# A graph network's edge stage on one core: rings and loop body of eight groups instead of four, the loads of P divided differently over two queues

## The reference

```
ef  = silu(concat(h[row], h[col], edge_attr) @ edge_w1 + edge_b1)
ef  = silu(ef @ edge_w2 + edge_b2)
agg = segment_sum(ef * edge_mask, row)
h   = h + (silu(concat(h, agg) @ node_w1 + node_b1) @ node_w2 + node_b2)
```

## Time and profile before

| | |
|---|---|
| median of 3 runs | 8981.45 us (8978.94 to 8988.67) |
| the profiled execution | 9007.83 us, span 9006.1 us |
| TensorE (PE) busy | 6678.6 us, 74% of the span |
| GpSimd (POOL) busy | 5100.8 us, 57% |
| VectorE (DVE) busy | 5014.9 us, 56% |
| ScalarE (ACT) busy | 2799.6 us, 31% |
| first and last `first` of L1 (L1515) | start at 2367.5 and 6357.6 us |

### The profile page before, as it was taken

The page is one execution under the profiler, slowest core; times in us unless marked ns, Lnnn a source line. Parts: engine busy times, 40 slices in busy tenths (PEclk is TensorE's granted clock), DMA queues, the critical chain, the costliest instruction groups (busy, mean ns, idle before and its releaser), DMA issues. The chain is left out here.

```text
span 9006.1 us, 230609 instructions
## 1 busy us (share of the span) xinstructions
PE 6678.6 (74%) x51782; PEld 5543.5 (62%) x51783; DVE 5014.9 (56%) x13561; ACT 2799.6 (31%) x8299; POOL 5100.8 (57%) x7138
## 2 busy tenths in 40 slices
PE   1222226767799978999799988999766666888998
PEld 1111114555577757777577767878455555786998
DVE  6333346867355545555455545555322222998999
ACT  1222204544233323333233322333133333222554
POOL 3777736755366636666366645666167776221554
PEclk8555555555799989999899999999655555998999
DMA  2000004433366646666455555666311000332232
GB/s 63 3 3 3 3 29 138 119 100 110 110 166 165 164 112 165 165 166 164 107 164 164 164 121 159 169 166 167 90 31 7 7 7 6 78 82 57 73 72 60
DMA packets 1288626, 877.60 MB, mean 97 GB/s; under 512 B 448518, under 2 KB 1192859, under 8 KB 1287640
## 3 DMA queue, kind: packets, MB, share of 16 engines
q1 hardware_dynamic: 991510, 618.55, 25.3%
q0 software_dynamic: 134272, 178.98, 9.3%
q10 hardware_dynamic: 162752, 78.98, 3.1%
HBM read 832.60 MB, written 50.91 MB: 98 GB/s over the span
## 5 line engine op out<-in xcount | busy, mean ns | idle before, releaser
L1472 POOL DMA_INDIRECT qg<-q_tab,qidx x2520 | 2393.5, 950 | 1444.0 <-DVE qidx L1602 736.5
L1607 DVE COPY ps<-b 128x384 f32<-128x384 f32 x1120 | 628.2, 561 | 1640.7 <-ACT h L1581 1609.1
L1067 PE MATMUL ps<-rhs_i,ohi 128*128 128x128 f32 (+2 forms) x8640 | 1215.1, 266 | 209.8 <-issue 198.0
L1067 PEld LDWEIGHTS ps<-rhs_i,ohi 128*128 128x128 f32 (+1 forms) x8640 | 998.8, 162 | 340.3 <-issue 281.2
L1033 POOL COPY near<-x 128x48 bf16 x2160 | 675.7, 351 | 788.4 <-PE ps L1056 432.9
L1542 PE MATMUL ps<-ohm,h 128*128 128x128 f32 x6720 | 1001.1, 285 | 146.6 <-DVE ps L1607 136.6
L1195 POOL DMA_INDIRECT got_m<-y_tab,idx_m x832 | 815.5, 980 | 474.2 <-issue 251.7
L1517 PE MATMUL ps<-oht,pb 128*128 128x128 f32 x6720 | 1060.5, 295 | 0.0
L1574 ACT ACTIVATE h<-ps,b 128x384 f32<-128x384 f32 x1120 | 650.2, 581 | 1292.6 <-PE ps L1522 1245.2
L1542 PEld LDWEIGHTS ps<-ohm,h 128*128 128x128 f32 x6720 | 842.0, 192 | 281.5 <-issue 275.7
L1581 ACT ACTIVATE h<-ps 128x384 f32<-128x384 f32 x1120 | 549.1, 490 | 1432.5 <-PE ps L1531 1343.5
(11 more groups left out here) (438 smaller groups left out, 8629.8 us busy)
## 6 DMA issues: line engine op xcount, KB each, us to landing
pb<-p_tab SPq DMA_DIRECT2D x2240, 64.0 KB
places<-place_by_turn SPq DMA_DIRECT2D x560, 192.0 KB
places_i<-place_by_meeting SPq DMA_DIRECT2D x360, 256.0 KB, 3.4
places_i<-place_by_meeting SPq DMA_DIRECT2D x720, 128.0 KB, 3.1
pb<-p_tab ACTq DMA_DIRECT2D x1120, 64.0 KB
qb<-q_tab SPq DMA_DIRECT2D x840, 64.0 KB
qg<-q_tab,qidx POOLq DMA_INDIRECT x2520
eat<-rows_by_turn SPq DMA_DIRECT2D x560, 54.0 KB
```

The lines of the kernel that those rows point to most:

```text
L1067: m = pe.matmul(ps[:, bass.ds(to[j], width)], ohi[:, h, j, :], rhs[:, h, j, 0:width], start=False, stop=True, skip_group_check=True)
L1472: pool.indirect_dma_start(qg[:, h, j, :], None, q_tab, IndirectOffsetOnAxis(ap=qidx[:, h, j:j + 1], axis=0)).then_inc(m_got[h], 16)
```

## The change

The rings of `edge_mlp` and its loop body get eight slots (`U3` = 8, 35 rounds instead of 70); the other stages keep `U` = 4. The waits follow: a load may run up to eight groups ahead. SP loads all three blocks of P of the even group of a pair, ScalarE all three of the odd one (before: four on SP, two on ScalarE), and ScalarE's `fetch` runs six groups ahead instead of two, with three fetches ahead of its first step. The indices are copied five groups ahead instead of three. `nears` is loaded for both groups of a pair in one transfer, also for the group that doesn't use it. TensorE's address load for `sums` moves out of `sums` to the head of the even step, ahead of `first`. The sizes and counts are those of before.

```diff
+U3 = 8
-K3 = G3 // U
+K3 = G3 // U3
...
-                return 3 if h == NONE else 2
+                return 3 if h % 4 == 3 else 2
+            def blocks(q):
+                return 2 - q % 2
...
-                qg = sb(f"qg{layer}", [P, U, M3, HID], F32, st)
-                pb = sb(f"pb{layer}", [P, U, M3, HID], F32, st)
+                qg = sb(f"qg{layer}", [P, U3, M3, HID], F32, st)
+                pb = sb(f"pb{layer}", [P, U3, M3, HID], F32, st)
...
@@ gpsimd, gather
-                            if here(k, h, U):
-                                pool.wait_ge(m_z1, g0 + n - U + 1)
+                            if here(k, h, U3):
+                                pool.wait_ge(m_z1, g0 + n - U3 + 1)
...
@@ sync, fetch
-                                sp.wait_ge(m_z1, g0 + n - 2)
+                                sp.wait_ge(m_z1, g0 + n - U3 + 2)
...
-                            for i in range(2 - q):
-                                sp.dma_start(nears[:, h + i, :], near_p[bass.ds((n + i) * M3 + 2, 1), :].to_broadcast([P, P])).then_inc(m_pl[q], 16)
+                            sp.dma_start(nears[:, h:h + 2, :],
+                                         near_p[bass.ds(n * M3, 2 * M3), :].rearrange("(a g j) p -> a g j p", a=1, j=M3)[:, :, 2, :].to_broadcast([P, 2, P])).then_inc(m_pl[q], 16)
...
-                            sp.dma_start(pb[:, h + 1, 0, :], p_tab[bass.ds(at[4], P), :]).then_inc(m_sp[q], 16)
...
@@ tensor
-                            pe.wait_ge(m_sp[q], 16 * (7 - q) * (k0 + k + 1))
-                            pe.wait_ge(m_act[q], 32 * (k0 + k + 1))
+                            pe.wait_ge(m_sp[q], 16 * (4 + blocks(q)) * (k0 + k + 1))
+                            if h % 2:
+                                pe.wait_ge(m_act[q], 48 * (k0 + k + 1))
...
@@ tensor, sums
-                            if h % 2 == 0:
-                                to[:] = address(mybir.EngineType.PE, to_p[0:1, bass.ds(k * 2 + h // 2, 1), :].rearrange("a g j -> a (g j)"), (NB - 1) * P)
...
+                        def take(k, h):
+                            to[:] = address(mybir.EngineType.PE, to_p[0:1, bass.ds(k * (U3 // 2) + h // 2, 1), :].rearrange("a g j -> a (g j)"), (NB - 1) * P)
...
                         def step(k, h):
+                            if h % 2 == 0 and here(k, h, 2):
+                                take(*moved(k, h, -2))
                             first(k, h)
...
@@ scalar, fetch
-                                act.wait_ge(m_z1, g0 + n - 2)
-                            at = address(mybir.EngineType.Activation, at_p[0:1, bass.ds(n + 1, 1), 1:3].rearrange("a g j -> a (g j)"), (NB - 1) * P)
-                            for j in range(2):
-                                act.dma_start(pb[:, h + 1, 1 + j, :], p_tab[bass.ds(at[j], P), :]).then_inc(m_act[q], 16)
+                                act.wait_ge(m_z1, g0 + n - U3 + 2)
+                            at = address(mybir.EngineType.Activation, at_p[0:1, bass.ds(n + 1, 1), 0:4].rearrange("a g j -> a (g j)"), (NB - 1) * P)
+                            for j in range(M3):
+                                act.dma_start(pb[:, h + 1, j, :], p_tab[bass.ds(at[j], P), :]).then_inc(m_act[q], 16)
...
@@ scalar, step
-                                fetch(*moved(k, h, 2))
-                        fetch(0, 0)
+                                fetch(*moved(k, h, 6))
+                        for h in (0, 2, 4):
+                            fetch(0, h)
...
@@ vector, step
-                            indices(*moved(k, h, U - 1))
+                            indices(*moved(k, h, 5))
```

More of the change, by code:

```diff
@@ L26 @@
 M3 = 3
+U3 = 8
 G3 = NT // M3
-K3 = G3 // U
+K3 = G3 // U3
 GW = M3 * P
-NONE = U - 1
-NA = K3 * NONE
+NA = G3 // 4 * 3
 assert NA <= NT - NB * (NB - 1)
@@ L925, in _, with turns @@
                         dve.tensor_copy(to_p[0:1, hs, 0:6], banks[3][0:1, 0:HN].rearrange("a (g j) -> a g j", j=6)).then_inc(c_blk, 1)
-        def turns(eng, step, rounds=K):
+        def turns(eng, step, rounds=K, ring=U):
             for k in (0, 1):
-                for h in range(U):
+                for h in range(ring):
                     step(k, h)
             with eng.Fori(2, rounds - 1) as k:
-                for h in range(U):
+                for h in range(ring):
                     step(k, h)
-            for h in range(U):
+            for h in range(ring):
                 step(rounds - 1, h)
@@ L1430, in gnn_kernel @@
             sem("m_" + n) for n in ("idx", "oht", "ohm", "z1", "h1", "z2", "h2", "sum", "seed"))
-        m_got = [sem(f"m_got{h}") for h in range(U)]
-        m_pl, m_sp, m_act = ([sem(f"m_{n}{q}") for q in range(2)] for n in ("pl", "sp", "act"))
+        m_got = [sem(f"m_got{h}") for h in range(U3)]
+        m_pl, m_sp, m_act = ([sem(f"m_{n}{q}") for q in range(U3 // 2)] for n in ("pl", "sp", "act"))
         Z1, Z2 = 3584, NP
@@ L1440, in here, with moved @@
             def here(k, h, lag=0):
-                return there(k, h, lag, G3)
+                return not isinstance(k, int) or lag <= k * U3 + h < G3
             def gathered(h):
-                return 3 if h == NONE else 2
-            with ExitStack() as st:
-                qidx = sb(f"qidx{layer}", [P, U, M3], I32, st)
-                qg = sb(f"qg{layer}", [P, U, M3, HID], F32, st)
-                pb = sb(f"pb{layer}", [P, U, M3, HID], F32, st)
[L1450 to L1455, removed]
+                return 3 if h % 4 == 3 else 2
+            def blocks(q):
+                return 2 - q % 2
+            def moved(k, h, by):
+                d, slot = divmod(h + by, U3)
+                return (k + d if d else k), slot
+            with ExitStack() as st:
+                qidx = sb(f"qidx{layer}", [P, U3, M3], I32, st)
+                qg = sb(f"qg{layer}", [P, U3, M3, HID], F32, st)
+                pb = sb(f"pb{layer}", [P, U3, M3, HID], F32, st)
+                qb = sb(f"qb{layer}", [P, U3, HID], F32, st)
+                places = sb(f"places{layer}", [P, U3, GW], BF16, st)
+                nears = sb(f"nears{layer}", [P, U3, P], BF16, st)
+                eat = sb(f"eat{layer}", [36, U3, GW], BF16, st)
+                oht = sb(f"oht{layer}", [P, U3, GW], F32, st)
+                ohn = sb(f"ohn{layer}", [P, U3, P], F32, st)
                 ohm = sb(f"ohm{layer}", [P, 2, M3, P], F32, st)
@@ L1473, in gather @@
                                                         IndirectOffsetOnAxis(ap=qidx[:, h, j:j + 1], axis=0)).then_inc(m_got[h], 16)
-                        turns(pool, gather, K3)
+                        turns(pool, gather, K3, U3)
                     @block.sync
@@ L1491, in fetch @@
                             at = address(mybir.EngineType.SP, at_p[0:1, bass.ds(n, 2), :].rearrange("a g j -> a (g j)"), (NB - 1) * P)
-                            for i in range(2 - q):
+                            for i in range(blocks(q)):
                                 sp.dma_start(qb[:, h + i, :], q_tab[bass.ds(at[4 * i + 3], P), :]).then_inc(m_sp[q], 16)
@@ L1495, in fetch @@
                                 sp.dma_start(pb[:, h, j, :], p_tab[bass.ds(at[j], P), :]).then_inc(m_sp[q], 16)
-                            sp.dma_start(pb[:, h + 1, 0, :], p_tab[bass.ds(at[4], P), :]).then_inc(m_sp[q], 16)
                         sp.wait_ge(c_three, 48)
-                        turns(sp, fetch, K3)
+                        turns(sp, fetch, K3, U3)
                     @block.tensor
@@ L1551, in step @@
                                 second(*moved(k, h, -1))
[L1552 to L1555, removed]
+                        turns(pe, step, K3, U3)
+                        take(K3 - 1, U3 - 2)
+                        sums(K3 - 1, U3 - 2)
+                        second(K3 - 1, U3 - 1)
+                        sums(K3 - 1, U3 - 1)
                     @block.scalar
@@ L1576, in two @@
                         def two(k, h):
-                            n = k * U + h
+                            n = k * U3 + h
                             if here(k, h, 2):
@@ L1587, in step @@
                             if h % 2 == 0:
-                                fetch(*moved(k, h, 2))
-                        fetch(0, 0)
-                        turns(act, step, K3)
-                        two(K3 - 1, U - 2)
-                        two(K3 - 1, U - 1)
+                                fetch(*moved(k, h, 6))
+                        for h in (0, 2, 4):
+                            fetch(0, h)
+                        turns(act, step, K3, U3)
+                        two(K3 - 1, U3 - 2)
+                        two(K3 - 1, U3 - 1)
                     @block.vector
@@ L1633, in step @@
                             build(*moved(k, h, 1))
-                            indices(*moved(k, h, U - 1))
+                            indices(*moved(k, h, 5))
                             if here(k, h, 1):
                                 build_m(*moved(k, h, -1))
-                        for h in range(U - 1):
```

(5 more changed lines are left out.)

38 lines of the change are left out of this document (19 added, 19 removed).

## The result

The changed kernel takes 9034.11 us (median of 4 runs, 9029.61 to 9043.84), the kernel before 8983.93 us beside it (4 runs, 8978.94 to 8988.67). The ratio is 1.0057, 95% interval 1.004 to 1.0075: 50 us slower. The forecast was 8954, 80 us less than measured.

What follows compares the result with a forecast made beforehand. TensorE, and what makes it wait, was taken to set the time. Steady rounds +16, layer ends -6 and -4, last groups -34 gave -28 us against the profiled 9007.83, carried over to the runs' median as 8954 us; range 8890 to 9070.

Steps and rivals of the forecast that it cites:

- the load and some 0.1 us of register work fit in ... I take 0: TensorE's moved address load, 0.59 us, behind `second`: covered by 1.53 us of matmuls, so cost 0.
- The bound of the prediction, 317 us: TensorE's moved load if its cover were gone: at most 0.6 us twice a round, over 264 rounds.
- the gain of 34 us in the last groups: Layer ends: four more slots let TensorE run on during slow gathers, 8.5 us a layer gained, -34 us.
- Longer rings, the wait of 0.60 us a round goes.: Steady rounds, slot 0: with eight slots `first` no longer waits for rows of P, 0.60 us a round.
- ScalarE's third row, 0.33 us for each of two waits a round, 174 us.: ScalarE's fetch: third issue +0.51 us, shorter load -0.18, so two waits of 0.33 us more a round.
- Steady rounds, 13.20 us.: Rounds of four groups: 13.14 - 0.60 + 2 x 0.33 = 13.20 us, 0.06 slower, 264 times: +16 us.
- Ends of the layers.: Last six steps have no fetch, -6 us; at layer starts SP issues two transfers fewer first, -4 us.
- the first rival: ScalarE's fetch grows by more than 0.33 us: by 0.51 gives 9048 us, by 0.65 gives 9122, slower; chance 0.25.
- the third: Longer loop body's code fetched anew each turn: up to 290 us, with half of it 9100 us, slower; chance 0.06.
- The second: Slow gathers near layer ends are not helped, the crowd is there whatever the ring: 8988 us, same; chance 0.12.
- The fourth: Lateness taken up: ScalarE's third issue doesn't hold `two` back, round 12.54 us, 8779 us in all, much faster; chance 0.10.

## Why the prediction was wrong

The step that failed is "the load and some 0.1 us of register work fit in ... I take 0", on the address load of TensorE that was moved ahead of `first`. The cover, 1.53 us of matmuls, was counted from the start of `sums`, as if the sequencer came to the load at that time. It comes there, in program order, only after it has sent off `second`: 0.5 to 0.7 us after the start of `sums` in slots 2, 4 and 6, and 1.0 us after it where the loop has jumped back. `first` starts 0.9 to 1.0 us after the load at the earliest. In slots 2, 4 and 6 that just fits; at the head it doesn't. There the interval is 0.40 us longer than with the load back (4.11 against 3.71 us in the first layer, 4.0 against 3.6 in the others), at 128 heads some 51 us, and undoing it gave 68 us by the ratios and 54 by the traces. The bound of the prediction, 317 us, was for all even slots; one in four of them pays, and pays two thirds of 0.6 us. That the jump back is what brings the sequencer to the load half a microsecond later is shown, since slot 0 of the turn written straight out has no such delay. What in the jump takes that time stays open: the records have only an ALU operation of 0.036 us just ahead of the load. It is no fetching of code, since the queues that bring instructions moved nothing from 2450 to 3250 us of the changed kernel. And without a load behind it the jump costs nothing that TensorE's matmuls don't cover.

The second step that failed is the gain of 34 us in the last groups; it is the fifth point below.

The rest, in the prediction's order:

- *Longer rings, the wait of 0.60 us a round goes.* Right; no `first` waits for a transfer in steady rounds. With the other two parts undone this is worth 1.9% of the kernel before, 166 us by the medians; 264 x 0.60 is 158, and the steady rounds of the two traces differ by 0.59 us. The 0.60 came out of a division that was a little off: a round without waits was put at 11.53 us, and where nothing waits (ScalarE's rows between `two` and `one`) it takes 11.65, because slot 3 takes 2.91 us too in spite of its missing pass. So the waits in `sums` had 0.89 us of a round and not 1.01.
- *ScalarE's third row, 0.33 us for each of two waits a round, 174 us.* Right in mechanism, and in size to a tenth or so: load 0.308, `two` 0.10 behind the issues (its three span 1.35 us), the wait of `sums` from 0.47 to 0.74, a round 0.59 us longer in the traces and not 0.66 (some 20 us less over 264), and 172 us when undone, 148 by the traces. The rule of the Trainium skill (DMA: Bandwidth & Descriptors, "Latency and other measured facts"), a floor of some 600 ns for such a load, does not hold here: it took 304 to 326 ns on ScalarE.
- *Steady rounds, 13.20 us.* The kernel with the load back has 13.25 in the first layer and 13.05 to 13.11 in the others, 13.13 in the mean: right, lower by what the third row cost less. With the wait at the head it is 13.32.
- *Ends of the layers.* The last four intervals are 3.02 us each, without the wait in `sums`, as forecast. The start was forecast to gain 4 us and lost 3: `first` waits 5.75, 4.75, 5.50 and 5.77 us for its first row of P, against 4.10, 5.22, 4.55 and 4.52. ScalarE now issues nine rows beside SP ahead of the first group, instead of two. Whether this makes SP's own row late is open: with both parts undone, where it issues six, the waits are 4.92 to 5.70 us, no shorter.
- *The last groups, -34 us.* Mis-sized. The intervals 6.01, 3.73, 10.74 and 3.34 us of the first layer stand for some 10.5 us lost. Over four layers the slow gathers cost 41 us here and 57 before (each kernel against itself with spread indices): a gain of 16 us and not 34. TensorE no longer waits for rows of P, as was said of the longer ring. But ScalarE's own issues were then held up for 7.14 us, and `two` is behind them. The prediction looked for the crowd in the transfers alone and not in the engine that issues them; the trace of before had no sign of it, since ScalarE's issues there took 0.39 us at most near a layer's end. Taking the slow gathers away gave 58 us by the ratios.

The terms put right make the forecast's 8954 to 8954 + 51 - 21 + 18 + 7 = 9009 us (head, third row, last groups, start), or 9026 with the 68 us that the ratios give for the head, against 9034 measured. The 8 to 25 us that are left have no term; the interval of the comparison alone is some 15 us either way. That 9034 lies between the prediction's 8890 and 9070 is luck: its upper part was reached by the first rival's cause, which didn't come.

Of the rivals, the third had the sign by a neighbouring mechanism, the turn's head, but not by its own: no code was fetched in the steady turns of the first layer, and the kernels with the load back have a body as long and no wait. The second was half right on the layers' ends. The first was wrong, and the load's 0.31 us is why. The fourth was wrong too: behind `one` the third row is paid in full. It is hidden only when the fetch stands where ScalarE has time.

One more reading was missing, and it was worth most. The prediction found that ScalarE's fetch sets the odd steps, and in the same rows that ScalarE is busy 31 to 32% of the time, with 1.08 us of waiting before `one`. It then priced how much longer the fetch gets, and never asked where else it could stand.

## What to carry to other kernels

Count the cover of an instruction that is moved from when its sequencer gets there to when the next instruction is needed, not from the start of the matmuls around it, and take the place behind a loop's jump back as one of its own: a load of 0.59 us that was free in three even slots of the body, and in slot 0 written straight out, cost 0.40 us there. When an engine that is 31% busy holds up the one that bounds the kernel, look first for the place in its step where it waits anyway: moving the three issues there gained 4.0%, taking one of them off the engine 1.7%. A crowd on the DMA engines is paid for at the data's reader or, when loads are asked for further ahead, at the engine that issues them, with all that stands behind; padding should not point to one row of a table.

## What the runs showed of the hardware

- A DMA issue, 0.35 us as a rule, can block its engine: three of ScalarE took 7.14 us while the gathers' queue had 70.1% of the DMA engines. A crowd alone doesn't do it: with 67.2% in the kernel before, none of ScalarE's issues took over 0.39 us near a layer's end. It came in the kernels that fetch further ahead, and went from the two of them that have spread indices (0.38 us at most). That the number of transfers still waiting in the queue decides is only an inference; no run varies it by itself.
- Behind a loop's jump back TensorE's sequencer came to its next instruction some 0.5 us later than in a turn written straight out (0.97 to 1.13 us after `sums` against 0.38 to 0.47); the matmuls already sent off hid that, but not an address load on top of it.
- Gathers of one and the same row take five times as long for each packet as gathers of spread rows (70.1% for 416 against 18.2% for 537 in 25 us each).
- Address loads took different times by engine and form: on ScalarE 0.31 us for four values from the first of four places on, and 0.49 for two from the second on the earlier trace rows; on TensorE 0.59 for eight values; on SP 0.69 for eight. Number and place of the values were not varied apart.
